# Attention of a metaformer layer: SyncE's loads put in another order, score tables in quarters, and the row maximum of three pieces in eight subtracted on GpSimd

## The chip, the cores and the metric

One core of one Trainium2 chip runs the whole layer as one program. The metric is the device time of one launch, in microseconds. Names of the engines in the profile: PE is TensorE's matmuls, PEld its weight loads, DVE is VectorE, ACT is ScalarE, POOL is GpSimd, SP is SyncE, whose queue issues nearly all transfers of this stage.

## What is computed

The layer normalises x over its last axis, adds an axial attention of 16 heads over the width, and adds a mixture of experts. The change is in the attention alone. For each of the 4 images, 16 heads and 128 rows i there is a 128 x 128 matrix of weights over j and w:

```
qk = jnp.einsum('nhcij,nhciw->nhijw', q, k) / D
qrq = jnp.einsum('nhcij,chjw->nhijw', q, rq) / D
krk = jnp.einsum('nhcij,chjw->nhijw', k, rk) / D
weight = jax.nn.softmax(qk + Gq * qrq + Gk * krk, axis=3)
out = jnp.einsum('nhijw,nhciw->nhcij', weight, Gv1 * v) + jnp.einsum('nhijw,chjw->nhcij', weight, Gv2 * rv)
```

The softmax runs over j. The tables rq, rk and rv belong to a head, so they change only when the head changes.

## The kernel before

Five stages run one after the other: prepare, project (it writes q, k and v to memory), attend (this case), combine, experts.

attend works in units. A unit is 64 rows of one image for one head, so a head has 8 units (k = 0 to 7) and there are 128 in all. A unit's scores lie in one of four buffers `scores0` to `scores3`, with w on the partitions. A unit is done in 8 turns (p = 0 to 7), one piece of 8 rows each, and several units are in hand at once. In a turn

- PE first does the own scores of piece p of unit u (`att_own`, L592), mixed with one round of relative scores from the tables (`att_rs` times `att_qk`, L581). These are for unit u + 1 while p < 6, and for unit u + 2 after that. Then come the sums with v (L622) and with rv (L634) for an earlier unit: u - 2 in turns 0 to 3, and u - 1 in turns 4 to 7;
- DVE adds the own scores to the relative ones and takes the row's extreme, negated (`add_and_largest`, L732, eight instructions). Two turns later it sums the exponentials of a piece (L715) and inverts the sums (L717);
- ACT takes exponentials of the piece before, row by row, with that row's `negmax` as its bias (`exp_half`, L675, eight instructions a piece). Then it copies the round of relative scores from PSUM into the buffer (`read_relative`, L668), and in every odd turn it copies a finished block of sums with rv out of PSUM (`read_r`, L682);
- POOL multiplies a piece by its inverse (`normalise`, L770).

The orders are written out by hand, and two waits matter most. PE's relative scores of a turn go into two banks of PSUM that ACT must have emptied (`rel_read`) before the next turn begins. `read_r` waits until PE has ended its odd turn (`r_done`).

SP issues in `unit` (L509 to L543): the second half of `att_own` for this unit, `att_qk` for two units ahead, the stores of unit u - 2, `att_vt` for unit u - 1, the first half of `att_own` for the next unit, and so on. PE needs the first `att_vt` at turn 4. In unit k = 6 SP also loads the next head's tables: 8 small loads of gains, then `att_rs` in two halves of 8 transfers each. A half can be overwritten only when PE has read it for unit 7. POOL multiplies each half by the gains (`scale_relative`, L765) before PE may use it. PE needs the first half at turn 6 of unit 6, and the second at turn 2 of unit 7.

Of the kernel before, what the change touches and what calls it, by code (L numbers as in the profile page):

```python
# [387 lines left out]
PR = 8  # L388
# [7 lines left out]
STORES_R = W // JT  # L396


def attend(nc, d):


    with ExitStack() as ctx:
# [12 lines left out]
        rs_loaded = [s.sem(f"rs_loaded{a}") for a in range(2)]  # L415
        rs_ready = [s.sem(f"rs_ready{a}") for a in range(2)]
# [8 lines left out]
        cleared = s.sem("cleared")  # L425
# [22 lines left out]
        def _(sp):  # L448
# [3 lines left out]
            def load_relative(h, a):  # L452
                for g in range(G):
                    for t in range(2):
                        at = slice(32 * g + HD * t, 32 * g + HD * t + HD)
                        j = g * JG + a * (JG // 2)
                        sp.dma_start(rs[at, a * (JG // 2):(a + 1) * (JG // 2), :].rearrange("c j w -> c (j w)"),
                                     tables[t][:, bass.ds(h, 1), j:j + JG // 2, :].rearrange("c h j w -> (c h) (j w)")).then_inc(rs_loaded[a], 16)
# [46 lines left out]
            def unit(h, k, u, started, left):  # L505
                if started >= 1:
                    sp.wait_ge(own_done, PIECES * u)
                    load_own(h, k, 1)
                if left >= 2:  # L509
                    sp.wait_ge(rel_done, ROUNDS * u + ROUNDS)  # L510
                    load_qk(*after(h, k, 2))
                if started >= 2:
                    store(*before(h, k, 2), u - 2, 0)
                if started >= 1:
                    ph, pk = before(h, k, 1)
# [6 lines left out]
                fresh = k == UPH - 2 and left >= 2  # L522
                if fresh:
                    load_gain(h + 1)
                    sp.wait_ge(rel_done, ROUNDS * u + ROUNDS + ROUNDS // 2)
                    load_relative(h + 1, 0)
                if left >= 1:
                    sp.wait_ge(own_done, PIECES * u + PIECES // 2)
                    load_own(*after(h, k, 1), 0)
                if started >= 1:  # L530
                    later(sp, v_done, FILLS * (u - 1))
                    load_v(ph, pk, 1)
                    if pk == 0:
                        later(sp, r_done, FILLS * (u - 1))
                        load_rv(ph, 2)
                        load_rv(ph, 3)
                if started >= 2:
                    store(*before(h, k, 2), u - 2, 1)
                if fresh:
                    sp.wait_ge(rel_done, ROUNDS * u + 2 * ROUNDS)  # L540
                    load_relative(h + 1, 1)

            load_gain(0)  # L543
            for a in range(2):
                load_relative(0, a)
# [3 lines left out]
            for half in range(2):  # L549
                load_own(0, 0, half)  # L550
            for k in range(UPH):
                unit(0, k, k, k, 2)
            with sp.Fori(1, NH - 1) as h:
                for k in range(UPH):
                    unit(h, k, UPH * h + k, 2, 2)
# [15 lines left out]
        def _(pe):  # L571
            def before_relative(u, v, t):
                if t == 0:
                    pe.wait_ge(qk_loaded[v % 2], 64 * (u // 2) + 64)
                if t % (ROUNDS // 2) == 0:
                    pe.wait_ge(rs_ready[t // (ROUNDS // 2)], u // UPH + 1)
                later(pe, rel_read, ROUNDS * u + t)
# [83 lines left out]
        def _(act):  # L661
# [15 lines left out]

            def read_r(u, b):
# [5 lines left out]
            def unit(u, v, parts):  # L684
                back2, back1, now, ahead1, ahead2 = parts
                for p in range(PIECES):
# [13 lines left out]
                    if p % 2 and p >= 4 and back1:  # L700
                        read_r(u - 1, p // 2 - 2)

# [57 lines left out]
        def _(pool):  # L760
            def scale_relative(h, a):
                half = slice(a * (JG // 2), (a + 1) * (JG // 2))
                pool.wait_ge(rs_loaded[a], 128 * h + 128)
                pool.wait_ge(gain_loaded, 128 * h + 128)
                pool.tensor_tensor(rs[:, half, :], rs[:, half, :], gain[:, :].unsqueeze(2).broadcast_to([P, JG // 2, W]), ALU.mult).then_inc(rs_ready[a], 1)  # L765
# [7 lines left out]
            def head(h, last):  # L773
                for k in range(UPH):
                    for p in range(PIECES):
                        if k == UPH - 2 and not last and p == 3:
                            scale_relative(h + 1, 0)
                        if k == UPH - 2 and not last and p == 7:
                            scale_relative(h + 1, 1)
                        normalise(UPH * h + k, k % BUFS, p)  # L780

            for a in range(2):
                scale_relative(0, a)
            with pool.Fori(0, NH - 1) as h:
                head(h, False)
            head(NH - 1, True)
# [553 lines left out]
```

## Time and profile before

| | |
|---|---|
| median of 3 runs | 7852.92 us (7848.76 to 7871.15) |
| the profiled execution | 7833.53 us, span of its instructions 7831.8 us |
| attend, first to last turn | 1575 to 6184 us of the span |
| busy over the span | PE 83%, PE's weight loads 64%, DVE 68%, ACT 60%, POOL 32% |

The profiled execution is 19 us below the median. The rows quoted later give the start in us from the start of the span, then the length in us, then engine, line, operation and tiles, and at the end in brackets how long the engine stood idle before and what ended that. Matmuls of one kind that follow each other are merged into one row with their count (two records for each matmul of the source). The relative and own scores alternate, so they make many short rows, of which only the first of a turn is shown.

### The profile page before, as it was taken

To read this page: it belongs to the slowest core of one execution; us is meant where nothing else is said; L and a number is where in the kernel's file an instruction comes from. 1 tells how busy PE (TensorE), PEld (TensorE's weight loads), DVE (VectorE), ACT (ScalarE), POOL (GpSimd) and SP (SyncE) were. 2 spreads that over 40 slices of the span, in tenths; PEclk is the share of its full clock that TensorE was granted. 3 is DMA by queue.
4 is the path that set the end of the run, shared out by engine and by line. 5 is a ranking of instruction groups with operands and counts; after the bars stand their busy time and mean duration, and the time that the engine had idled before them with its cause. 6 is when DMAs were issued, how large, how long until landed. Compare 5 with 4: busy or idle time off the path is not lost. (4 is left out here: it accounts for less than half of the span.)

```text
span 7831.8 us, 282296 instructions
## 1 busy us (share of the span) xinstructions
PE 6488.4 (83%) x106442; PEld 5044.5 (64%) x106442; DVE 5358.1 (68%) x20905; ACT 4715.2 (60%) x11171; POOL 2470.2 (32%) x1235
## 2 busy tenths in 40 slices
PE   4999999788898888888898888888888776675648
PEld 3555555477777777777777777777777632232248
DVE  5444444267787777777777777777777698888830
ACT  0444444277787787787787787787787533343310
POOL 0000000034444444444444444444444432232210
PEclk7999999879999999999999999999999998897855
DMA  7555555546656566666656656666666686686522
GB/s 220 202 204 203 203 204 202 147 90 119 117 114 121 112 116 118 114 115 120 113 114 121 114 113 122 112 115 120 111 115 120 148 266 194 202 263 198 177 92 91
DMA packets 1861132, 1148.19 MB, mean 147 GB/s; under 512 B 1162209, under 2 KB 1623649, under 8 KB 1853601
## 3 DMA queue, kind: packets, MB, share of 16 engines
q1 hardware_dynamic: 1670368, 842.63, 49.2%
q10 hardware_dynamic: 188352, 285.27, 10.0%
q8 instruction: 834, 13.66, 0.8%
q14 instruction: 554, 4.53, 0.2%
q0 software_dynamic: 1024, 2.09, 0.1%
HBM read 708.04 MB, written 421.56 MB: 144 GB/s over the span
## 5 line engine op out<-in xcount | busy, mean ns | idle before, releaser
L770 POOL TENSOR_TENSOR att_scores<-att_scores,att_inverse 128x1024 f32<-128x1024 f32 x1024 | 1989.5, 1943 | 2452.0 <-DVE att_inverse L717 2452.0
L732 DVE CUSTOM_DVE_ANT_0 att_scores<-att_ps,att_scores 128x128 f32<-128x128 f32 x8192 | 1819.2, 289 | 1158.7 <-PE att_ps L592 1120.5
L675 ACT ACTIVATE att_scores<-att_scores,att_negmax 128x128 f32<-128x128 f32 x8192 | 2515.0, 394 | 74.7 <-issue 69.5
L581 PE MATMUL att_ps<-att_qk,att_rs 32*128 32x64 f32 x32768 | 2253.6, 300 | 50.8 <-DMA att_qk<-qk 40.5
L592 PE MATMUL att_ps<-att_own 32*128 32x128 f32 x16384 | 1859.1, 328 | 401.3 <-POOL att_rs L765 179.4
L592 PEld LDWEIGHTS att_ps<-att_own 32*128 32x128 f32 x16384 | 1657.3, 197 | 712.4 <-issue 463.3
L581 PEld LDWEIGHTS att_ps<-att_qk,att_rs 32*128 32x128 f32 x32768 | 2073.5, 200 | 52.8 <-issue 43.6
L668 ACT ACTIVATE att_scores<-att_ps 128x1024 f32<-128x1024 f32 x1024 | 1033.7, 1010 | 609.3 <-PE att_ps L581 608.6
L634 PE MATMUL att_ps<-att_scores,att_rv 128*16 128x64 f32 x32768 | 1384.5, 332 | 9.3 <-DMA att_rv<-rv_t 6.3
L715 DVE TENSOR_REDUCE att_total<-att_scores 128x8 f32<-128x1024 f32 x1024 | 1241.5, 1212 | 0.0
L634 PEld LDWEIGHTS att_ps<-att_scores,att_rv 128*16 128x16 f32 x32768 | 1130.9, 121 | 35.1 <-DMA att_rv<-rv_t 12.1
L366 PE MATMUL proj_qk_ps<-proj_xn,proj_w_qk 128*128 128x512 f32 x2048 | 902.5, 594 | 33.4 <-DVE proj_xn L230 33.4
L622 PE MATMUL att_ps<-att_scores,att_vt 128*16 128x128 f32 x16384 | 692.2, 290 | 214.1 <-DMA att_vt<-v_t 182.6
L890 PE MATMUL comb_y_ps<-comb_att,comb_wo 128*128 128x512 f32 x1024 | 510.9, 657 | 220.9 <-DVE comb_x L931 193.5
L366 PEld LDWEIGHTS proj_qk_ps<-proj_xn,proj_w_qk 128*128 128x128 f32 x2048 | 390.2, 191 | 470.3 <-issue 463.8
L732 DVE DVE_READ_ACCUMULATOR2_ANT att_negmax<- 128x1 f32 x8192 | 688.6, 84 | 0.1
L335 ACT ACTIVATE proj_qk_out<-proj_qk_ps 128x512 f32<-128x512 f32 x512 | 305.1, 596 | 625.7 <-PE proj_qk_ps L366 616.7
L765 POOL TENSOR_TENSOR att_rs<-att_rs,att_gain 128x2048 f32<-128x2048 f32 x32 | 115.3, 3604 | 1640.4 <-DMA att_rs<-in_L_conv_rk_dram 1640.4
L622 PEld LDWEIGHTS att_ps<-att_scores,att_vt 128*16 128x16 f32 x16384 | 374.7, 99 | 336.3 <-issue 218.1
L872 POOL TENSOR_TENSOR comb_att<-comb_sum_v,comb_sum_r 128x1024 f32<-128x1024 f32 x128 | 329.0, 2590 | 819.9 <-DMA comb_x<-in_x_dram 739.2
L890 PEld LDWEIGHTS comb_y_ps<-comb_att,comb_wo 128*128 128x128 f32 x1024 | 209.6, 210 | 527.0 <-issue 274.2
L682 ACT ACTIVATE att_att_r<-att_ps 128x512 f32<-128x512 f32 x512 | 305.8, 597 | 370.1 <-PE att_ps L634 370.0
(147 smaller groups left out, 5173.6 us busy)
## 6 DMA issues: line engine op xcount, KB each, us to landing
qk<-proj_qk_out ACTq DMA_DIRECT2D x64, 2048.0 KB, 8.6
att_qk<-qk SPq DMA_DIRECT2D x512, 256.0 KB, 5.9
att_own<-qk SPq DMA_DIRECT2D x2048, 64.0 KB, 2.5
proj_x<-in_x_dram SPq DMA_DIRECT2D x128, 512.0 KB, 4.3
v_t<-proj_v_out ACTq DMA_DIRECT2D x64, 1024.0 KB, 11.7
att_vt<-v_t SPq DMA_DIRECT2D x256, 256.0 KB, 3.3
att_v<-att_att_v SPq DMA_DIRECT2D x1024, 64.0 KB, 2.5
att_r<-att_att_r SPq DMA_DIRECT2D x1024, 64.0 KB, 2.1
```

The costliest lines, as they stand in the source:

```text
L366: last = pe.matmul(qk_ps[:, j], w_qk[:, a, 4 * j:4 * j + 4].rearrange("c h t e -> c (h t e)"), xn[u][:, a, sub * BANK:(sub + 1) * BANK], s ...
L581: return pe.matmul(ps[:, 4 + gg, jj * IU:(jj + 1) * IU], rs[32 * g:32 * g + 32, j, :], qk[v % 2][32 * g:32 * g + 32, :, j], start=True, st ...
L592: return pe.matmul(ps[:, g, r * W:(r + 1) * W], own[half][32 * g:32 * g + 32, 1, at, :], own[half][32 * g:32 * g + 32, 0, at, :], start=Tr ...
L622: last = pe.matmul(ps[32 * g:32 * g + HD, 6, r * W:(r + 1) * W], vt[i // HROWS][:, i % HROWS, :], scores[v % BUFS][:, i, :], start=True, s ...
L634: last = pe.matmul(ps[32 * g:32 * g + HD, 7, jj * IU:(jj + 1) * IU], rv[:, j, :], scores[v % BUFS][:, :, j], start=True, stop=True, tile_p ...
L668: act.activation(scores[o % BUFS][:, :, :].rearrange("w i (g j) -> w i g j", g=G)[:, :, pair:pair + 2, t // 2 * JB:(t // 2 + 1) * JB], ps[ ...
L675: last = act.activation(scores[v % BUFS][:, i, :], scores[v % BUFS][:, i, :], ACT.Exp, bias=negmax[v % BUFS][:, i:i + 1], scale=-1.0)
L715: dve.tensor_reduce(total[v][:, rows], scores[v][:, rows, :], AX_X, ALU.add).then_inc(summed, 1)
L732: last = dve.tensor_tensor_reduce(out=scores[v][:, i, :], in0=ps[:, 2 * (p % 2) + r // HR, (r % HR) * W:(r % HR + 1) * W], in1=scores[v][: ...
L770: pool.tensor_tensor(scores[v][:, rows, :], scores[v][:, rows, :], inverse[v][:, rows].unsqueeze(2).broadcast_to([P, PR, W]), ALU.mult).th ...
L872: pool.tensor_tensor(att[u][:, a, :].rearrange("c (i g j) -> c i g j", i=ROWS, g=STORES_R), sum_v[u][:, a, :].rearrange("c (i g j) -> c i ...
L890: last = pe.matmul(y_ps[:, b], wo[:, a, o * P:(o + 1) * P], att[u][:, a, sub * BANK:(sub + 1) * BANK], start=a == 0, stop=a == CHALF - 1)
```

## The change

It has three parts.

1. In SP's order the first `att_vt` comes right behind the first `att_own`, ahead of the stores. `att_qk` moves from the start of the unit to its end, and is loaded for three units ahead.
2. The tables come in quarters, each loaded as soon as PE has done with the old one, and each multiplied by the gains on its own.
3. For pieces 0, 2 and 4 of every unit POOL subtracts the scores from the row extreme (`shift`), and ACT then takes one exponential over the whole piece (`exp_shifted`) in place of eight. These come at the end of ACT's turn, behind `read_r`. POOL's `normalise` runs two pieces behind.

```diff
@@ sync: unit
+                ahead = ROUNDS * (u + 1)
+                fresh = k == UPH - 2 and left >= 2
                 if started >= 1:
+                    ph, pk = before(h, k, 1)
                     sp.wait_ge(own_done, PIECES * u)
                     load_own(h, k, 1)
-                if left >= 2:
-                    sp.wait_ge(rel_done, ROUNDS * u + ROUNDS)
-                    load_qk(*after(h, k, 2))
-                if started >= 2:
-                    store(*before(h, k, 2), u - 2, 0)
                     later(sp, v_done, FILLS * (u - 2) + FILLS // 2)
                     load_v(ph, pk, 0)
...
                 if fresh:
                     load_gain(h + 1)
-                    sp.wait_ge(rel_done, ROUNDS * u + ROUNDS + ROUNDS // 2)
+                    sp.wait_ge(rel_done, ahead + 2)
                     load_relative(h + 1, 0)
+                if started >= 2:
+                    store(*before(h, k, 2), u - 2, 0)
+                if fresh:
+                    sp.wait_ge(rel_done, ahead + 4)
+                    load_relative(h + 1, 1)
...
+                if left >= 3:
+                    sp.wait_ge(rel_done, ahead + ROUNDS)
+                    load_qk(*after(h, k, 3))
@@ scalar
+            def exp_shifted(u, v, p):
+                rows = slice(p * PR, (p + 1) * PR)
+                act.wait_ge(shifted, len(SHIFTED) * u + SHIFTED.index(p) + 1)
+                act.activation(scores[v % BUFS][:, rows, :], scores[v % BUFS][:, rows, :], ACT.Exp, scale=-1.0).then_inc(exped, 2)
...
-                    elif now:
+                    elif now and p - 1 not in SHIFTED:
                         exp_half(u, v, 2 * p - 2)
                         exp_half(u, v, 2 * p - 1)
...
+                    if now and p - 1 in SHIFTED:
+                        exp_shifted(u, v, p - 1)
@@ gpsimd
+            def shift(u, v, p):
+                rows = slice(p * PR, (p + 1) * PR)
+                pool.wait_ge(added, HALVES * u + 2 * p + 2)
+                pool.tensor_tensor(scores[v][:, rows, :], scores[v][:, rows, :], negmax[v][:, rows].unsqueeze(2).broadcast_to([P, PR, W]),
+                                   ALU.subtract).then_inc(shifted, 1)
+            def head(h, first, last):
+                for k in range(UPH):
+                    u = UPH * h + k
                     for p in range(PIECES):
+                        if k == UPH - 2 and not last and p % 2 == 1:
+                            scale_relative(h + 1, p // 2)
+                        if p in SHIFTED:
+                            shift(u, k % BUFS, p)
+                        if p >= BEHIND:
+                            normalise(u, k % BUFS, p - BEHIND)
+                        elif k or not first:
+                            normalise(u - 1, (k - 1) % BUFS, PIECES + p - BEHIND)
```

ACT's order in unit 2, whose scores are `att_scores2`, from the `read_r` (L682) of turn 1 to that of turn 3. Before:

```order
L682 ACTIVATE att_att_r1<-att_ps 128x64x8
L675 ACTIVATE att_scores2<-att_scores2,att_negmax2 128x128 x8
L668 ACTIVATE att_scores3<-att_ps 128x64x2x8
L675 ACTIVATE att_scores2<-att_scores2,att_negmax2 128x128 x8
L668 ACTIVATE att_scores3<-att_ps 128x64x2x8
L682 ACTIVATE att_att_r1<-att_ps 128x64x8
```

And in the changed kernel, where `read_r` is L697, `exp_half` L685, `read_relative` L678 and `exp_shifted` L691:

```order
L697 ACTIVATE att_att_r1<-att_ps 128x64x8
L691 ACTIVATE att_scores2<-att_scores2 128x1024
L685 ACTIVATE att_scores2<-att_scores2,att_negmax2 128x128 x8
L678 ACTIVATE att_scores3<-att_ps 128x64x2x8 x2
L697 ACTIVATE att_att_r1<-att_ps 128x64x8
```

Before, one group of eight exponentials stood in each turn, ahead of its `read_relative`. Now both exponentials of a pair of turns stand between `read_r` and the `read_relative` of the even turn, and none stands in the odd turn.

POOL in unit 6, from the first to the last multiplication of the tables (L782), where L787 is `normalise` and L793 `shift`, in the changed kernel:

```order
L782 TENSOR_TENSOR att_rs<-att_rs,att_gain 128x1024
L787 TENSOR_TENSOR att_scores<-att_scores,att_inverse 128x1024
L793 TENSOR_TENSOR att_scores<-att_scores,att_negmax 128x1024
L787 TENSOR_TENSOR att_scores<-att_scores,att_inverse 128x1024
L782 TENSOR_TENSOR att_rs<-att_rs,att_gain 128x1024
L787 TENSOR_TENSOR att_scores<-att_scores,att_inverse 128x1024
L793 TENSOR_TENSOR att_scores<-att_scores,att_negmax 128x1024
```

Before, POOL had two such multiplications of 128 x 2048 in this unit, in turns 3 and 7, and only `normalise` around them; now there are four of 128 x 1024, in turns 1, 3, 5 and 7, and the `shift` of pieces 2 and 4 stands behind the first two.

## Rows read from the trace of the kernel before

**Rows 1.** ACT in a regular stretch, order of time (turn pair without stall).

```profile
2721.09 0.60 ACT L682 ACTIVATE att_att_r<-att_ps 128x512 f32<-128x512 f32 x1 [0.71 <-PE att_ps L634]
2721.58 2.47 ACT L675 ACTIVATE att_scores<-att_scores,att_negmax 128x128 f32<-128x128 f32 x8
2723.95 1.00 ACT L668 ACTIVATE att_scores<-att_ps 128x1024 f32<-128x1024 f32 x1
2724.85 2.43 ACT L675 ACTIVATE att_scores<-att_scores,att_negmax 128x128 f32<-128x128 f32 x8
...
2728.92 0.60 ACT L682 ACTIVATE att_att_r<-att_ps 128x512 f32<-128x512 f32 x1 [0.73 <-PE att_ps L634]
```

**Rows 2.** PE in the same stretch: sums with v (L622), with rv (L634).

```profile
2719.68 1.35 PE L634 MATMUL att_ps<-att_scores,att_rv 128*16 128x64 f32 x32
...
2723.39 1.34 PE L634 MATMUL att_ps<-att_scores,att_rv 128*16 128x64 f32 x32
2725.00 0.37 PE L592 MATMUL att_ps<-att_own 32*128 32x128 f32 x1 [0.28 <-ACT att_scores L668]
...
2726.97 0.63 PE L622 MATMUL att_ps<-att_scores,att_vt 128*16 128x128 f32 x16
2727.42 1.35 PE L634 MATMUL att_ps<-att_scores,att_rv 128*16 128x64 f32 x32
```

**Rows 3.** Waits in attend, 1575 to 6184: us in total, times, longest.

```profile
PE att_ps L622 <- DMA att_vt<-v_t: 182.1, 74, 4.4
PE att_ps L592 <- POOL att_rs L765: 179.4, 30, 9.3
PE att_ps L592 <- ACT att_scores L668: 127.5, 362, 1.2
```

**Rows 4.** SP's queue in a unit 6: start, time to issue, count.

```profile
2654.75 4.17 SPq L477 DMA_DIRECT2D att_own<-qk  x7
2659.20 6.61 SPq L469 DMA_DIRECT2D att_qk<-qk  x4
...
2672.37 0.38 SPq L482 DMA_DIRECT2D att_vt<-v_t  x1
2672.93 3.62 SPq L464 DMA_DIRECT2D att_gain<-gain_t  x8
2676.80 0.32 SPq L457 DMA_DIRECT2D att_rs<-in_L_conv_rq_dram  x1
...
2681.40 0.37 SPq L457 DMA_DIRECT2D att_rs<-in_L_conv_rk_dram  x1
```

**Rows 5.** POOL in the same unit.

```profile
2686.55 3.60 POOL L765 TENSOR_TENSOR att_rs<-att_rs,att_gain 128x2048 f32<-128x2048 f32 x1 [7.88 <-DMA att_rs<-in_L_conv_rk_dram]
```

**Rows 6.** PE in the same unit: start of turn 3, then of turn 6.

```profile
2667.70 0.37 PE L592 MATMUL att_ps<-att_own 32*128 32x128 f32 x1 [0.26 <-ACT att_scores L668]
...
2690.29 0.57 PE L592 MATMUL att_ps<-att_own 32*128 32x128 f32 x1 [8.09 <-POOL att_rs L765]
...
2693.90 1.05 PE L622 MATMUL att_ps<-att_scores,att_vt 128*16 128x128 f32 x16
```

**Rows 7.** Groups of instructions, 1400 to 6600: count | busy us, mean ns | idle before.

```profile
L770 POOL TENSOR_TENSOR att_scores<-att_scores,att_inverse 128x1024 f32<-128x1024 f32 x1024 | 1989.5, 1943 | 2452.0 <-DVE att_inverse L717 2452.0
...
L668 ACT ACTIVATE att_scores<-att_ps 128x1024 f32<-128x1024 f32 x1024 | 1033.7, 1010 | 609.3 <-PE att_ps L581 608.6
...
L205 ACT ACTIVATE comb_ln_sq<-comb_ln_xc 128x2048 f32<-128x2048 f32 x19 | 36.3, 1910 | 88.7 <-DVE comb_ln_xc L201 86.2 <-issue 2.3
```

**Rows 8.** PE behind a wait of 1.25 us for v.

```profile
5541.72 0.63 PE L622 MATMUL att_ps<-att_scores,att_vt 128*16 128x128 f32 x16 [1.25 <-DMA att_vt<-v_t]
...
5545.41 0.63 PE L622 MATMUL att_ps<-att_scores,att_vt 128*16 128x128 f32 x16
```

**Rows 9.** PE behind a wait of 1.52 us for v.

```profile
4601.29 0.80 PE L622 MATMUL att_ps<-att_scores,att_vt 128*16 128x128 f32 x16 [1.52 <-DMA att_vt<-v_t]
...
4606.00 0.63 PE L622 MATMUL att_ps<-att_scores,att_vt 128*16 128x128 f32 x16
```

More of the change, by code:

```diff
@@ L414, in attend @@
         ps = s.ps("ps", [P, 8, BANK])
-        rs_loaded = [s.sem(f"rs_loaded{a}") for a in range(2)]
-        rs_ready = [s.sem(f"rs_ready{a}") for a in range(2)]
+        rs_loaded = [s.sem(f"rs_loaded{a}") for a in range(QUARTERS)]
+        rs_ready = [s.sem(f"rs_ready{a}") for a in range(QUARTERS)]
         qk_loaded = [s.sem(f"qk_loaded{b}") for b in range(2)]
@@ L536, in unit @@
                         load_rv(ph, 3)
+                if fresh:
+                    sp.wait_ge(rel_done, ahead + 6)
+                    load_relative(h + 1, 2)
                 if started >= 2:
@@ L539, in unit @@
                 if fresh:
-                    sp.wait_ge(rel_done, ROUNDS * u + 2 * ROUNDS)
-                    load_relative(h + 1, 1)
+                    sp.wait_ge(rel_done, ahead + 8)
+                    load_relative(h + 1, 3)
+                if left >= 3:
+                    sp.wait_ge(rel_done, ahead + ROUNDS)
+                    load_qk(*after(h, k, 3))
             load_gain(0)
-            for a in range(2):
+            for a in range(QUARTERS):
                 load_relative(0, a)
@@ L550, in _ @@
                 load_own(0, 0, half)
+            sp.wait_ge(rel_done, ROUNDS)
+            load_qk(0, 2)
             for k in range(UPH):
[L552 removed]
+                unit(0, k, k, k, 3)
             with sp.Fori(1, NH - 1) as h:
                 for k in range(UPH):
[L555 removed]
+                    unit(h, k, UPH * h + k, 2, 3)
             for k in range(UPH):
@@ L771, in normalise @@
                                    ALU.mult).then_inc(normed, 1)
-            def head(h, last):
+            def shift(u, v, p):
[3 more added lines that the diff above has]
+                                   ALU.subtract).then_inc(shifted, 1)
+            BEHIND = 2
+            def head(h, first, last):
                 for k in range(UPH):
+                    u = UPH * h + k
                     for p in range(PIECES):
[L776 to L782, printed above, removed]
-                scale_relative(0, a)
-            with pool.Fori(0, NH - 1) as h:
-                head(h, False)
-            head(NH - 1, True)
+                        if k == UPH - 2 and not last and p % 2 == 1:
[6 more added lines that the diff above has]
+                            normalise(u - 1, (k - 1) % BUFS, PIECES + p - BEHIND)
+            for a in range(QUARTERS):
+                scale_relative(0, a)
+            head(0, True, False)
+            with pool.Fori(1, NH - 1) as h:
+                head(h, False, False)
+            head(NH - 1, False, True)
+            for p in range(PIECES - BEHIND, PIECES):
+                normalise(UNITS - 1, (UPH - 1) % BUFS, p)
 def combine(nc, d):
```

21 lines of the change are left out of this document (10 added, 11 removed).

## Prediction

> **What bounds the kernel now.** The change touches attend alone, 4,609 of 7,832 us, so I read that stage turn by turn. In a regular pair of turns ACT's timeline shows this order [rows 1]: `read_r` at 2721.09, exponentials at 2721.58, `read_relative` at 2723.95, exponentials at 2724.85, and `read_r` again at 2728.92, for which it waited 0.73 us for PE. PE's timeline shows the other side [rows 2]: its sums with rv start at 2719.68, 2723.39 and 2727.42. So the odd turn gives way to the even one after 3.71 us, and the even one to the next after 4.03 us. At 2725.00, which begins the next turn, PE had waited 0.28 us for ACT's `read_relative`. The reader is to see a loop of two engines: PE ends an odd turn, ACT does `read_r`, the exponentials and `read_relative`, and only then may PE begin the turn after next. The start of `read_r` to the end of `read_relative` is 2724.95 - 2721.09 = 3.86 us. A bit over 0.1 us at the two hand-overs, and PE's turn of 3.70 us, fit under the same roof, so both engines are nearly bound, and it matters on which side of `read_r` a piece of ACT's work stands.
>
> A unit without stalls is four pairs of 4.06 + 3.70 us, or 31.1 us, and 128 of them 3,980 us. The stage takes 4,609. The list of waits says where most of the rest goes [rows 3]: PE waited 182 us in 74 places for `att_vt`, and 179 us in 30 places for the tables. Each longer wait costs more than itself. After one for the tables PE is at the lower of its two clock levels, 1.2 GHz where it has 2.4 otherwise: the scores of the turn take 2693.90 - 2690.29 = 3.61 us [rows 6], where 2726.97 - 2725.00 = 1.97 us is regular [rows 2], and with the sums with v behind them the turn is about 2.0 us longer. After a wait of 1.52 us for v the sums with v follow each other at 4.71 us [rows 9], 1.0 us over the 3.69 that a wait of 1.25 us left behind it [rows 8].
>
> **Part 1, SP's order.** SP is a serial queue that takes time to issue. In a unit 6 [rows 4] `att_own` is issued by 2659.2, then `att_qk` takes 6.6 us, the stores take until 2672.4, and only then `att_vt` goes, at 2672.37. Without the 13 us between, it goes at 2659.2, 13 us sooner, and the longest wait for it was 4.4 us. I take all of the 182 us as gone, and with them the slow scores, about 65 us (some 65 of the 74 waits at 1.0 us, an estimate from rows 8 and 9). Gain: 247 us. What becomes late instead: `att_qk` goes at turn 5 and is used at turn 6 of the next unit, over 30 us later. The stores are needed a unit later. SP's issues of a regular unit come to at most 30 us (twice `att_own` at 4.7, `att_qk` at 6.6, twice the stores at up to 6.6, 0.8 for v, all from rows 4), below its 31 to 34 us. I count nothing.
>
> **Part 2, tables in quarters.** The first quarter can be overwritten before unit 6 begins, and goes behind `att_own`, `att_vt` and the gains. From the times in rows 4 I take out the 13.2 us of `att_qk` and stores: gains at 2659.7, the quarter issued from 2663.6 to some 2668, landed by 2670.2 to 2673.3 (POOL got the half 5.1 us after the last issue [rows 4, 5]; the quarter has half the bytes, so 2.2 to 5.1). PE needs it only at turn 6, 17 us on. The three others come one to every two turns, each with as much room. The 179 us go, and with them 30 slow turns at 2.0 us, 60. Gain: 239 us.
>
> POOL, though, is an engine with one order. The multiplication of the first quarter stands in turn 1, and behind it wait one `normalise` and the `shift` of piece 2. With 1.94 us for each operation on 128 x 1024 [rows 7] the three end 5.8 us behind the landing, between 2676.0 and 2679.1. ACT wants it after `read_r` of turn 3: that turn began at 2667.70 before [rows 6], 0.93 us later now (below), and 3.7 + 0.5 us bring it to 2672.8. So ACT, and PE behind it, stand 3.2 to 6.3 us in every unit 6. I take 3.2, the near end, since these loads then have the transfers to themselves, and 1.0 us for the slow scores behind it: 15 x 4.2 = 63 us back. The GPSIMD Engine Reference of the Trainium skill, section 3.1, measures 4.50 us for a two-input operation of 2048 elements; here 3.60 us is measured [rows 5], and the measurement decides. By the page's figure three operations at half would take 6.7 us in place of 5.8, and the sum would be 14 us higher. Sixteen more issues by SP at the start of the stage, about 0.5 us each, are partly under the transfers: 4 us.
>
> **Part 3, the wide exponential.** ACT's work falls: eight exponentials take 2.37 us from start to start [rows 1], and one over 1024 elements should take about 0.93 us. I take the copy of 1024 elements, 1.01 us long and 0.90 to the next start [rows 1, 7]; half of the square over 2048 with its fixed part, also 1.04 us [rows 7], less 0.1 of overlap, gives 0.94. Ends: 0.85 and 1.05. Three pieces save 4.3 us of ACT in a unit.
>
> But ACT is not short of time where these pieces go. They leave the odd turn, where ACT then only waits longer for PE, and come to stand behind `read_r`, ahead of the exponentials and the `read_relative` that PE waits for. The path from PE's end of an odd turn to its start of the turn after next grows from 4.06 by the whole wide exponential to 4.99 us, in turns 2, 4 and 6. PE's wait there grows from 0.28 to 1.21 us. Nothing covers it: PE's work in the turn is 3.70 us. The saved 2.37 us lie in turns that PE bounds at 3.70, and give nothing. So 3 x 0.93 x 127 units = 354 us are lost (ends 324 and 400). The `shift` itself adds 3 x 1.94 us to POOL's 8 x 1.94, under 22 of 34 us. Outside unit 6 it waits only for DVE's addition of the same turn, and ACT wants it at the end of the next, so some 2 us of room are left and it costs nothing; without that room its own 1.94 us would be on the path, up to the hold of unit 6.
>
> **The clock.** Will 381 new waits of 1.21 us bring PE's clock down? A wait of 1.25 us did not: the next turn is 3.69 us [rows 8]. One of 1.52 us did [rows 9]. The new one is under this line by little, and it lies beside the scores and not between scores and sums. I take one in four as followed by a lower level, at 0.3 us each, since most of the slow work then falls into the next wait: 30 us. Ends: 0, and one in two at 0.6, 114 us. The Trainium skill, TensorE: Matmul & The Clock Gate, in the section on a second failure mode (psum-queue depth-cycling), says that frequent short idles of PE between groups, without one long idle, make the clock go up and down. That speaks against this change, and by that rule the costly end would hold.
>
> **Sum.** -247 - 239 + 63 + 4 + 354 + 30 = -35 us. That is 7,799 us against the profiled execution's 7,833.5. The runs' median is 19 us above it, so 7,853 - 35 = 7,818; I round to 7,815.
>
> **The rivals.**
>
> - *The wide exponential is not exposed.* If ACT's loop has slack that I don't see, or the wide one takes much less, the transfers' gain shows: -35 - 354 + part. With half exposed it is 7,640, with nothing exposed 7,460. For it: the transfers' stalls are large and real. Against it: the 0.28 us that PE waits already [rows 2]. Chance 0.10.
> - *The clock falls at the new waits.* One in two at 0.6 us gives 114 in place of 30 us: 7,900. At 1.0 us for every second, as behind the wait of 1.52 us, it is 7,978. Slower from the point where the mean cost of a new wait passes 0.17 us (65/381). Chance 0.16.
> - *POOL's order holds ACT longer in unit 6.* At 6.3 us in place of 3.2 it costs 47 us more: 7,862, no difference. It becomes slower only with a second hold in the same unit. Chance 0.10.
> - *The loads are not earlier* because SP or the transfer engines are full. If half of the waits for v stay, it is +120 us: 7,935. Against it: the 13 us of room. Chance 0.04.
> - The forecast, 7,740 to 7,875: 0.60.
>
> **How the numbers follow.** 0.3% is 24 us, about what can be told from no change. In the forecast's own range, two thirds lie below -24 us, most of the rest within it. Faster: 0.60 x 0.66 + 0.10 = 0.50. Slower: 0.16 + 0.04 + 0.02 + a few hundredths of the forecast = 0.25. Same: 0.25. The range from 7,725 to 7,910 leaves out the first rival and the worst of the second and fourth, about 2 in 10.
>
> **What would show it.** Right: PE's rows for v follow each other at 4.99 and 3.70 us in turns 2 to 7; PE's wait for `read_relative` ahead of the own scores goes from 127 us in total [rows 3] to nearly 500; waits for `att_vt` and the tables are gone; POOL waits for the table's load in turn 1 of unit 6, and ACT for POOL two turns on; ACT's busy time is down by 500 us with no gain from it. Wrong: even turns at 4.06 us, a granted clock in regular units that is well under 1.00, or a new wait on a DMA in units 6 and 7.

## The result, and the profile after it

The changed kernel takes 7925.77 us (median of 4 runs, 7911.08 to 7927.84), the kernel before in the same session 7850.84 us (4 runs, 7842.32 to 7871.15). The ratio is 1.0088, interval 1.0065 to 1.0111: 75 us slower by the medians, where 35 us faster was forecast, and 16 us above the end of the stated range. Attend alone moved: from 4609.5 us to 4691.2 us in the profiled executions. The page's line of busy times, after:

```profile
PE 6529.8 (83%) x106442; PEld 5094.0 (64%) x106442; DVE 5360.0 (68%) x20905; ACT 4212.9 (53%) x8483; POOL 3177.3 (40%) x1651
```

ACT works 502 us less than before (4715.2) and POOL 707 us more (2470.2), and neither shows in the time. The list of waits in attend, 1575 to 6266 (us in total, times, longest), answers to [rows 3]:

```profile
PE att_ps L602 <- ACT att_scores L678: 517.0, 456, 4.4
...
POOL att_rs L782 <- DMA att_rs<-in_L_conv_rk_dram: 228.9, 60, 10.3
PE att_ps L602 <- issue: 108.6, 29, 4.7
ACT att_scores L691 <- POOL att_scores L793: 82.7, 25, 6.7
...
PE att_ps L632 <- POOL att_scores L787: 25.6, 12, 3.6
...
PE att_ps L602 <- DMA att_own<-qk: 0.5, 1, 0.5
```

The first column is the total, the second the number of waits. The waits for `att_vt` (182 us) and for the multiplied tables (179 us) are gone. PE's wait for `read_relative` went from 127.5 to 517.0 us. ACT now waits for `shift`, 82.7 us. PE in a regular stretch, the sums with rv (L644) and the first own scores of a turn, answers to [rows 2]:

```profile
2679.33 1.34 PE L644 MATMUL att_ps<-att_scores,att_rv 128*16 128x64 f32 x32
2680.95 0.37 PE L602 MATMUL att_ps<-att_own 32*128 32x128 f32 x1 [0.28 <-ACT att_scores L678]
...
2683.38 1.35 PE L644 MATMUL att_ps<-att_scores,att_rv 128*16 128x64 f32 x32
...
2687.08 1.35 PE L644 MATMUL att_ps<-att_scores,att_rv 128*16 128x64 f32 x32
2689.68 0.37 PE L602 MATMUL att_ps<-att_own 32*128 32x128 f32 x1 [1.25 <-ACT att_scores L678]
...
2692.10 1.34 PE L644 MATMUL att_ps<-att_scores,att_rv 128*16 128x64 f32 x32
```

Turn 0 of unit 6 still has the old order: from its sums with rv (2679.33) to those of the next turn (2683.38) it is 4.05 us, with the old wait of 0.28 us between. From turn 2, the next even one, with a wide exponential (2687.08), it is 5.02 us (2692.10), with a wait of 1.25 us. ACT in the same stretch and on through the stall of unit 6, which answers to [rows 1] (`read_r` L697, `exp_shifted` L691, `exp_half` L685, `read_relative` L678):

```profile
2684.79 0.60 ACT L697 ACTIVATE att_att_r<-att_ps 128x512 f32<-128x512 f32 x1 [0.71 <-PE att_ps L644]
2685.28 1.05 ACT L691 ACTIVATE att_scores<-att_scores 128x1024 f32<-128x1024 f32 x1
2686.23 2.49 ACT L685 ACTIVATE att_scores<-att_scores,att_negmax 128x128 f32<-128x128 f32 x8
2688.60 1.03 ACT L678 ACTIVATE att_scores<-att_ps 128x1024 f32<-128x1024 f32 x1
2691.77 1.02 ACT L678 ACTIVATE att_scores<-att_ps 128x1024 f32<-128x1024 f32 x1 [2.14 <-PE att_ps L591]
2693.51 0.60 ACT L697 ACTIVATE att_att_r<-att_ps 128x512 f32<-128x512 f32 x1 [0.72 <-PE att_ps L644]
2700.83 1.08 ACT L691 ACTIVATE att_scores<-att_scores 128x1024 f32<-128x1024 f32 x1 [6.72 <-POOL att_scores L793]
```

From `read_r` at 2684.79 to the end of `read_relative` at 2689.63 it is 4.84 us, where it was 3.86. In the odd turn ACT now idles 2.14 us: most of the 2.37 us that were saved there, used by nobody. Then comes the hold that was forecast at 3.2 us. It is 6.72 us long here, the longest of the heads 1 to 14, which have 3.3 to 6.7 us and 5.2 in the mean. What led to it stands in SP's queue and on POOL:

```profile
2668.84 6.04 SPq L471 DMA_DIRECT2D att_qk<-qk  x4
2675.22 7.06 SPq L479 DMA_DIRECT2D att_own<-qk  x8
2682.53 0.35 SPq L484 DMA_DIRECT2D att_vt<-v_t  x1
2683.05 4.70 SPq L466 DMA_DIRECT2D att_gain<-gain_t  x8
2688.04 0.32 SPq L459 DMA_DIRECT2D att_rs<-in_L_conv_rq_dram  x1
...
2691.66 1.11 SPq L459 DMA_DIRECT2D att_rs<-in_L_conv_rk_dram  x1
```

```profile
2695.11 1.89 POOL L782 TENSOR_TENSOR att_rs<-att_rs,att_gain 128x1024 f32<-128x1024 f32 x1 [10.27 <-DMA att_rs<-in_L_conv_rk_dram]
2696.96 1.90 POOL L787 TENSOR_TENSOR att_scores<-att_scores,att_inverse 128x1024 f32<-128x1024 f32 x1
2698.82 1.93 POOL L793 TENSOR_TENSOR att_scores<-att_scores,att_negmax 128x1024 f32<-128x1024 f32 x1
```

`att_qk` now stands right ahead of the own load of the next unit. Here the eight issues of `att_own` take 7.06 us, where seven took 4.17 [rows 4], and the gains take 4.70 for 3.62. Over the stage, the eight issues of `att_own` right behind `att_qk` take 6.3 us in the middle (42 places, with 8 of 10 between 5.7 and 7.2), and 4.1 us right behind `att_vt` in the kernel before (66 places). PE begins its next turn at 2705.20, after 4.02 us without work.

To add this up I took, for each turn, the time from its first own scores to those of the next turn, as a mean over heads 1 to 14, by unit (k) and turn. Before and after, the units that matter:

```
        turn 0     1     2     3     4     5     6     7
before k2  4.06  3.70  4.05  3.70  7.08  3.98  4.15  3.69
after  k2  4.07  3.70  5.03  3.81  5.03  3.78  5.10  3.71
before k3  4.06  3.70  4.05  3.70  6.21  4.24  4.15  6.95
after  k3  4.09  3.70  5.03  3.77  5.02  3.76  5.10  7.25
before k6  4.06  3.70  4.05  3.70  6.27 13.30  5.74  3.88
after  k6  4.07  3.70  5.02  3.96 10.34  5.57  5.09  3.75
before k7  4.05  7.17  4.89  3.98  4.06  3.70  4.15  6.99
after  k7  4.14  3.70  5.60  4.56  4.93  3.77  5.10  7.87
before k0  4.35  3.99  4.13  3.70  4.21  3.70  4.15  3.69
after  k0  5.53  4.18  5.10  3.96  5.03  3.76  5.09  3.83
```

Summed over a head it is 289.85 us before and 295.36 after, 5.5 us more. By parts, in us a head: waits for v -15.6; tables -16.0; wide exponential +23.1 (24 even turns at 0.95 to 0.98); turns 4 and 5 of unit 6 +7.2; turns 2 to 4 of unit 7 +1.3; the turns at the jumps of the loop (turn 7 of units 3 and 7, turns 0 and 1 behind them) +2.7; small excesses of other turns, most of them odd turns behind a wait of 1.2 us, +2.7.

### The profile page after: what moved, and what is told of

Same layout as the page of the kernel before. It is cut to its first block and busy times, and to the rows that moved or that the text cites. A ratio compares the mean times of both kernels' runs of the same rounds, so it can differ in the third digit from the quotient of the medians.

```text
span 7909.4 us, 281112 instructions
## 1 busy us (share of the span) xinstructions
PE 6529.8 (83%) x106442; PEld 5094.0 (64%) x106442; DVE 5360.0 (68%) x20905; ACT 4212.9 (53%) x8483; POOL 3177.3 (40%) x1651
## 3 DMA queue, kind: packets, MB, share of 16 engines
q0 software_dynamic: 1024, 2.09, 0.1%
## 5 line engine op out<-in xcount | busy, mean ns | idle before, releaser
L787 POOL TENSOR_TENSOR att_scores<-att_scores,att_inverse 128x1024 f32<-128x1024 f32 x1024 | 1987.0, 1942 | 1449.1 <-DVE att_inverse L734 1449.0
L602 PE MATMUL att_ps<-att_own 32*128 32x128 f32 x16384 | 1890.8, 332 | 627.9 <-ACT att_scores L678 517.0
L591 PE MATMUL att_ps<-att_qk,att_rs 32*128 32x64 f32 x32768 | 2292.8, 303 | 50.5 <-DMA att_qk<-qk 39.9
L602 PEld LDWEIGHTS att_ps<-att_own 32*128 32x128 f32 x16384 | 1688.6, 200 | 943.2 <-ACT att_scores L678 633.9
L591 PEld LDWEIGHTS att_ps<-att_qk,att_rs 32*128 32x128 f32 x32768 | 2112.4, 204 | 52.7 <-issue 46.2
L685 ACT ACTIVATE att_scores<-att_scores,att_negmax 128x128 f32<-128x128 f32 x5120 | 1580.1, 398 | 80.9 <-issue 80.4
L678 ACT ACTIVATE att_scores<-att_ps 128x1024 f32<-128x1024 f32 x1024 | 1038.4, 1014 | 1042.4 <-PE att_ps L591 1042.2
L644 PE MATMUL att_ps<-att_scores,att_rv 128*16 128x64 f32 x32768 | 1383.7, 332 | 1.9 <-ACT att_att_r L697 1.9
L644 PEld LDWEIGHTS att_ps<-att_scores,att_rv 128*16 128x16 f32 x32768 | 1140.2, 122 | 20.6 <-issue 3.1
L793 POOL TENSOR_TENSOR att_scores<-att_scores,att_negmax 128x1024 f32<-128x1024 f32 x384 | 730.6, 1903 | 277.8 <-DVE att_negmax L749 274.5
L782 POOL TENSOR_TENSOR att_rs<-att_rs,att_gain 128x1024 f32<-128x1024 f32 x64 | 122.5, 1914 | 1740.1 <-DMA att_rs<-in_L_conv_rk_dram 1740.1
L922 PEld LDWEIGHTS comb_y_ps<-comb_att,comb_wo 128*128 128x128 f32 x1024 | 210.0, 210 | 520.7 <-issue 269.0
L697 ACT ACTIVATE att_att_r<-att_ps 128x512 f32<-128x512 f32 x512 | 306.0, 598 | 431.2 <-PE att_ps L644 431.2
```

What stands on the lines that cost most here:

```text
L591: return pe.matmul(ps[:, 4 + gg, jj * IU:(jj + 1) * IU], rs[32 * g:32 * g + 32, j, :], qk[v % 2][32 * g:32 * g + 32, :, j], start=True, st ...
L602: return pe.matmul(ps[:, g, r * W:(r + 1) * W], own[half][32 * g:32 * g + 32, 1, at, :], own[half][32 * g:32 * g + 32, 0, at, :], start=Tr ...
L644: last = pe.matmul(ps[32 * g:32 * g + HD, 7, jj * IU:(jj + 1) * IU], rv[:, j, :], scores[v % BUFS][:, :, j], start=True, stop=True, tile_p ...
L678: act.activation(scores[o % BUFS][:, :, :].rearrange("w i (g j) -> w i g j", g=G)[:, :, pair:pair + 2, t // 2 * JB:(t // 2 + 1) * JB], ps[ ...
L685: last = act.activation(scores[v % BUFS][:, i, :], scores[v % BUFS][:, i, :], ACT.Exp, bias=negmax[v % BUFS][:, i:i + 1], scale=-1.0)
L787: pool.tensor_tensor(scores[v][:, rows, :], scores[v][:, rows, :], inverse[v][:, rows].unsqueeze(2).broadcast_to([P, PR, W]), ALU.mult).th ...
```

## The experiments

"Head" is the sum over a head as above. Each ratio is to the kernel before in the same session, with its interval. The kernel before had a median of 7850.84 us beside the changed kernel, 7840.49 beside e1 to e4, 7841.73 beside e5 to e8, and 7837.36 beside e9 to e11. So where two versions of different sessions are compared, the text takes the difference of each from the kernel before of its session.

| run | median us | ratio | head us | regular turns 2, 4, 6 |
|---|---|---|---|---|
| before | 7837 to 7851 | 1 | 289.85 | 4.05 |
| changed kernel | 7925.77 | 1.0088 (1.0065 to 1.0111) | 295.4 | 5.03 |
| e1 | 7642.19 | 0.9739 (0.9717 to 0.9762) | 278.4 | 4.06 |
| e2 | 8069.65 | 1.0280 (1.0255 to 1.0306) | 305.5 | 5.03 |
| e3 | 7682.48 | 0.9792 (0.9770 to 0.9814) | 280.5 | 4.25 |
| e4 | 7932.76 | 1.0111 (1.0088 to 1.0135) | 296.4 | 5.03 |
| e5 | 7899.96 | 1.0075 (1.0060 to 1.0090) | 294.4 | 5.03 |
| e6 | 7597.28 | 0.9687 (0.9673 to 0.9700) | 275.8 | 4.05 |
| e7 | 7567.80 | 0.9649 (0.9634 to 0.9663) | 274.3 | 3.70 |
| e8 | 7642.44 | 0.9737 (0.9722 to 0.9752) | 278.3 | 4.05 |
| e9 | 7483.81 | 0.9550 (0.9529 to 0.9571) | 269.0 | 3.70 |
| e10 | 7501.28 | 0.9570 (0.9542 to 0.9597) | 268.6 | 4.05 |
| e11 | 7821.90 | 0.9982 (0.9969 to 0.9994) | 289.4 | 5.03 |

### Transfers alone, the exponential alone

e1 is the changed kernel with no shifted piece, so all exponentials are eight narrow ones again:

```diff
-SHIFTED = (0, 2, 4)
+SHIFTED = ()
```

> The changed kernel without its third part: no piece is shifted on GpSimd, all exponentials are again row by row in their old place, the order of SyncE and the quarters stay. Theory (the wide exponential stands on the path from read_r to read_relative): even turns are back at 4.06 us, the waits for v and the tables stay away, only GpSimd's hold in unit 6 is left. 7926 - 370 (three times 0.97 us in 127 units) - some 40 of slow scores behind the new waits, up to 100 less if the hold of unit 6 goes with the shift: 7,420 to 7,520 us. Rival (the transfers gave little, the time is lost in units 6 and 7 and in the order of SyncE): 7,800 or more.

Measured: 7642.19 us, 198 us faster than before, and so 273 us better than the changed kernel, which is 75 us slower. The even turns are back at 4.06 us. It missed its range, since turn 3 of unit 7 takes 12.39 us and turn 4 of unit 6 takes 9.75. The waits of e1 say for what:

```profile
POOL att_rs L782 <- DMA att_rs<-in_L_conv_rk_dram: 364.1, 60, 13.1
...
PE att_ps L602 <- DMA att_own<-qk: 128.1, 15, 10.9
...
PE att_ps L632 <- POOL att_scores L787: 83.2, 15, 6.8
```

The wait for `att_own` is new. It is 0.5 us in the changed kernel, whose longer turns give SP time.

e2 is the other half: the kernel before with the shift and the wide exponentials. With them go `normalise` two pieces behind, as in the change, and the two multiplications of the table halves two turns later (turn 5 of unit 6 and turn 1 of unit 7). Only ACT's part of the edit is shown:

```diff
+SHIFTED = (0, 2, 4)
-                    elif now:
+                    elif now and p - 1 not in SHIFTED:
+                    if now and p - 1 in SHIFTED:
+                        exp_shifted(u, v, p - 1)
```

> The kernel before with the third part alone: pieces 0, 2 and 4 are shifted on GpSimd and get one wide exponential at the end of ScalarE's turn; SyncE's order and the tables in halves are those of before. Theory: 7851 + 370 + some 40 for slow scores, 8,220 to 8,270 us, even turns at 5.03 us. Rival (the parts hide each other, the new wait is taken up in the waits for v): below 8,100 us, since the waits for v at turn 4 would take in the later turns.

Measured: 8069.65 us, 229 us slower than before, below the expected range and where the rival put it. The even turns are 5.03 us long. The wait for `att_vt` fell to 80 us from 182, since longer turns gave that load more time; turn 4 of unit 1 was 3.2 us over its regular length before and is 1.8 over it here. Alone the halves are -198 and +229 us, which adds up to +31, and together they are +75. A part of what each load gains by coming sooner, the longer turns give it anyway.

### The wide exponential on the other side of `read_r`

In e3 only the place in the turn changes:

```diff
+                    if now and p - 1 in SHIFTED:
+                        exp_shifted(u, v, p - 1)
                     if p % 2 and p < 4 and back2:
                         read_r(u - 2, 2 + p // 2)
                     if p % 2 and p >= 4 and back1:
                         read_r(u - 1, p // 2 - 2)
-                    if now and p - 1 in SHIFTED:
-                        exp_shifted(u, v, p - 1)
```

> The changed kernel with the wide exponential moved ahead of read_r in the same turn; its length and GpSimd's work stay. Theory (its place costs, not its length): ScalarE has about 0.65 us free ahead of read_r, so only some 0.3 us of each 0.95 stay on the path. Even turns 4.35 us in place of 5.03: 7926 - 381 x 0.67 - some of the slow scores = 7,640 to 7,680 us. Rival (GpSimd's extra work, or the shift that comes late, slows the turns): 7,900 us, since both are as before.

Measured: 7682.48 us, 158 us faster than before, and so 233 us better than the changed kernel. That is 2 us above the expected range. ACT in e3:

```profile
2458.82 1.02 ACT L678 ACTIVATE att_scores<-att_ps 128x1024 f32<-128x1024 f32 x1 [2.15 <-PE att_ps L591]
2459.74 1.13 ACT L691 ACTIVATE att_scores<-att_scores 128x1024 f32<-128x1024 f32 x1
2460.78 0.57 ACT L697 ACTIVATE att_att_r<-att_ps 128x512 f32<-128x512 f32 x1
2461.26 2.47 ACT L685 ACTIVATE att_scores<-att_scores,att_negmax 128x128 f32<-128x128 f32 x8
```

The wide exponential lies where ACT stood idle for PE. `read_r` starts without idle time ahead of it, so it is still some 0.2 us late: the turn takes 4.25 us, not 4.05. The same instructions, moved by one place, are worth 233 us.

### Removing the stall of unit 6

In e4 POOL multiplies each quarter two turns later, behind the `shift` that ACT needs:

```diff
-                        if k == UPH - 2 and not last and p % 2 == 1:
-                            scale_relative(h + 1, p // 2)
+                        if k == UPH - 2 and not last and p in (3, 5, 7):
+                            scale_relative(h + 1, p // 2 - 1)
+                        if k == UPH - 1 and not last and p == 1:
+                            scale_relative(h + 1, 3)
```

> The changed kernel with GpSimd's four multiplications of the tables each two turns later (turns 3, 5 and 7 of unit 6, turn 1 of unit 7). Theory (GpSimd waits for the first quarter's load with the shift of piece 2 queued behind it): the wait in turn 4 of unit 6 (10.3 us against 5.0) and the slow turn behind it go, 7926 - 15 x 7 = 7,820 us, and about 20 less if the longer turns 2 and 3 of unit 7 go too. Rival (ScalarE waits there for the load or the stores themselves): no difference, 7,926 us.

Measured: 7932.76 us, 92 us slower than before where the changed kernel is 75 slower: no gain, and not the 7,820 that was expected. Turn 4 of unit 6 is 5.02 us for 10.34, so the hold is gone; and turn 3 of unit 7 is 12.26 us for 4.56. SP's queue in e4, from the end of the last quarter:

```profile
2715.22 0.37 SPq L459 DMA_DIRECT2D att_rs<-in_L_conv_rk_dram  x1
2715.77 6.83 SPq L471 DMA_DIRECT2D att_qk<-qk  x4
2722.79 4.46 SPq L479 DMA_DIRECT2D att_own<-qk  x8
```

And PE waits for that last load:

```profile
2730.05 0.57 PE L602 MATMUL att_ps<-att_own 32*128 32x128 f32 x1 [8.70 <-DMA att_own<-qk]
```

In this head (head 3) the issues of that load end 56.5 us after the start of unit 6, and 56.0 us after it in the changed kernel, so SP is no later. PE comes to the load 50.6 us after that start in place of 60.3: the hold of unit 6 had given SP the time in which it caught up. In units 6 and 7 of the changed kernel, from issue to issue with no gap over 0.45 us, SP works for 78.6 of 81.2 us (mean of 14 heads). In the kernel before it was 72.6 of 83.7 us. SP is nearly full in these two units, and a stall that is removed in one place comes up at the next load.

e5 is e4 with the last quarter and `att_qk` of unit 6 issued in unit 7, behind the loads that are needed first:

```diff
+                if behind:
+                    sp.wait_ge(rel_done, ahead)
+                    load_relative(h + 1, 3)
+                    load_qk(*after(h, k, 2))
...
-                if fresh:
-                    sp.wait_ge(rel_done, ahead + 8)
-                    load_relative(h + 1, 3)
-                if left >= 3:
+                if left >= 3 and not fresh:
```

> As the run with the multiplications of the tables two turns later, and the last quarter of the tables and att_qk of unit 6 now go in unit 7, behind its att_own and att_vt. Theory (SyncE's queue is what is short in units 6 and 7: with the hold on GpSimd gone, att_own of unit 7 comes too late because the last quarter and att_qk stand ahead of it): the turn of 12.3 us and the slow one behind it go, 9.6 us in each of 15 heads, 7933 - 144 = 7,770 to 7,800 us. Rival (the transfers themselves are what is full there, and another one comes late in its place): 7,900 us or more.

Measured: 7899.96 us, 58 us slower than before, some 34 us better than e4 where 130 or more was expected, and so where the rival put it. Turns 3, 4 and 5 of unit 7 take 7.17, 8.02 and 5.22 us, now because the last quarter is late: POOL waits 8.14 us for it in the same head, and PE waits 43.4 us in 14 places for POOL's product. Another order helps a full queue little. e6 and e7 are e5 with no shifted piece, and with pieces 1, 3 and 5 in place of 0, 2 and 4. Then the wide exponential stands in the even turn, ahead of the odd turn's group of eight, where ACT is idle, and not between `read_r` and `read_relative`:

```diff
-SHIFTED = (0, 2, 4)
+SHIFTED = ()  # e6
...
+SHIFTED = (1, 3, 5)  # e7
```

> The same order of SyncE and of the tables, without the shift and the wide exponential. Theory: the transfers alone are then worth what was forecast for parts 1 and 2, since both long turns of the run with the transfers alone go (6.4 and 11.0 us over a regular turn pair, 15 heads, 260 us): 7642 - 260 = 7,380 to 7,410 us. Rival (one of the two stays or moves): 7,450 to 7,550 us.

> The same again with the shift and the wide exponential, but for pieces 1, 3 and 5 in place of 0, 2 and 4: the wide exponential then ends the even turn, where ScalarE is not behind read_r, and read_relative of the even turn comes right behind read_r. Theory (what counts is how much ScalarE has to do between read_r and the read_relative of the next turn): turns 2, 4 and 6 go from 4.05 us to PE's own 3.7 to 3.8, 7390 - 127 x 1.0 = 7,250 to 7,290 us. Rival (VectorE, whose work of a pair of turns is 7.1 to 7.4 us, bounds the turns then, or GpSimd's shift comes too late): 7,370 us or more.

Measured: 7597.28 and 7567.80 us, both slower than expected: e6 lies above both its range and its rival's, e7 where its rival put it. In e7 turns 2, 4 and 6 take 3.70 us, PE's own work, and turns 3, 5 and 7 take 3.75. So wide exponentials can shorten the loop of ACT and PE. Of the 127 us that this was to bring, e7 won 29 against e6, and the rest is given back: turn 3 of unit 7 takes 13.03 us and turn 5 of unit 6 11.25, and ACT waits 257.8 us for `shift`.

### The jump of the loop

The loops of PE, ACT and DVE hold four units and jump back after units 3 and 7. There PE waits for nothing that the profile shows ("issue"): 93.2 us in 29 places before, 108.6 after, and the longest went from 3.5 to 4.7 us. The moved `att_qk` is in flight just then. e8 is e6 with `att_qk` at the start of the unit again, behind v (in unit 6 behind the first quarter):

```diff
+                if left >= 2 and not fresh:
+                    sp.wait_ge(rel_done, ahead)
                     load_qk(*after(h, k, 2))
...
-                if left >= 3 and not fresh:
-                    sp.wait_ge(rel_done, ahead + ROUNDS)
-                    load_qk(*after(h, k, 3))
```

> As the run with the reordered SyncE and no shift, but att_qk goes for two units ahead near the start of the unit, behind att_own and att_vt, where it does not run beside the jump back of PE's and ScalarE's loops. Theory (att_qk at the end of the unit slows the fetch of instructions behind the jump: the turn is 8.0 us there against 6.95 before): turn 7 of units 3 and 7 is back at 7.0 us, 28 x 1.0 and some slow scores less: 30 to 45 us below the other run. Rival (the longer turn has another cause): no difference.

Measured: turn 7 of unit 3 went from 7.92 (e6) to 7.19 us, the longest wait of this kind from 4.8 to 3.8 us. Turn 7 of unit 7, whose `att_qk` moved too, stayed at 7.43 us. As a whole e8 is 45 us slower than e6, where 30 to 45 us faster was expected, since `att_qk` is ahead of loads and stores that are needed sooner: ACT's wait for the store of `att_r` grows from 44.0 to 177.0 us. So at one of the two jumps 0.7 us went with the transfers beside it, and the other did not change. What ends these waits the profile does not show.

### Fewer transfers

e9 is the changed kernel with pieces 1, 3 and 5 shifted, as in e7, and the tables in two halves, 16 transfers a head in place of 32. The second half and `att_qk` of unit 6 go at the end of unit 6, and not in unit 7 as in e7. The gains are loaded in unit 2. That is 24 issues less in units 6 and 7. POOL still multiplies by quarters, behind the `shift`s:

```diff
-                        j = g * JG + a * JB
+                        j = g * JG + a * HALF
...
-                pool.wait_ge(rs_loaded[a], 128 * h + 128)
+                pool.wait_ge(rs_loaded[a // 2], 128 * h + 128)
...
+            SCALED = ((UPH - 2, 3), (UPH - 2, 4), (UPH - 2, 7), (UPH - 1, 0))
```

e10 is e9 without shifted pieces, and e11 is e9 with the pieces 0, 2 and 4 of the change.

> As the changed kernel, with pieces 1, 3 and 5 shifted; the tables are loaded in two halves again (16 transfers a head in place of 32), the first behind the stores and the second behind turn 5 of unit 6; the gains are loaded in unit 2; GpSimd multiplies quarters, in turns 3, 4 and 7 of unit 6 and turn 0 of unit 7, behind the shift. Theory (SyncE issues without a break over units 6 and 7, some 0.5 us for each transfer, and whatever stands last comes late): with 24 issues less in these two units the long turns of 11 to 13 us go. The run with pieces 1, 3 and 5 and the quarters had 21.5 us of excess in units 6 and 7 of each head; all gone is 7568 - 320 = 7,250 us, and half of it 7,400. Rival (the loads are late since the transfer engines are full there, or the multiplications hold the shift): 7,500 us or more.

> The same order of transfers without shift and wide exponential. Theory: parts 1 and 2 are then worth what the forecast gave them, 7850 - 470 = 7,370 to 7,420 us. Rival (SyncE's issues are not what is short): 7,550 us or more, as the two runs without a shift and with quarters (7,642 and 7,597).

> The same order of transfers with pieces 0, 2 and 4 shifted and the wide exponential behind read_r, as in the changed kernel. Theory: the place of the wide exponential costs 3 x 0.97 us in 127 units whatever the transfers do, and some 40 us of slow scores: 7,400 + 370 + 40 = 7,780 to 7,820 us. Rival (without late transfers to share with, the wide exponential costs less): below 7,700 us.

Measured: 7483.81, 7501.28 and 7821.90 us. e10 lies between its range and its rival's, e11 2 us above its range. e9 is the fastest: 354 us faster than before. The waits that are left in it:

```profile
PE att_ps L598 <- POOL att_rs L778: 66.4, 15, 7.7
PE att_ps L598 <- DMA att_own<-qk: 62.6, 24, 6.5
ACT att_scores L687 <- POOL att_scores L789: 57.0, 23, 4.3
```

Against e7, e9 won 80 us, where 168 to 318 was expected. Its units are shorter, and the same loads are late in more places (turn 3 of unit 3 takes 6.96 us, turn 5 of unit 6 8.46). SP is still full: it works for 72.9 of the 74.4 us of units 6 and 7. Between e9 and e10 there is no clear difference: the medians are 17 us apart, the runs overlap (7474.55 to 7494.22 and 7481.40 to 7506.47), and the sums over a head are 269.0 and 268.6 us. Three turns of each unit are 0.35 us shorter in e9 (some 8 us a head), and all of it goes into the late loads.

e11 differs from the changed kernel only in the transfers and in POOL's order of the multiplications, and is 90 us better (15 us faster than before, where the changed kernel is 75 us slower). The other pairs say the same: 80 us from e7 to e9 and 92 us from e6 to e10, though there the order in unit 7 changes too. No run separates the halves from the gains that moved to unit 2. e11 differs from e10 only in the shifted pieces, and is 321 us slower: the even turns alone are 24 x 0.97 us a head longer, or 370 us, and part of the holds of e10 is covered by the longer turns (turn 5 of unit 6 takes 6.28 us in e10 and 3.79 in e11).

## Why the prediction was wrong

**The main terms were right.** Waits for v and slow turns behind them: forecast -247, measured -15.6 x 16 = -250. Tables: -239, measured -16.0 x 15 = -240. The wide exponential behind `read_r` is exposed in full: forecast +354 at 0.93 us, measured +366 at 0.96 in the mean, and e3 and e11 show that it is the place and not the instruction that costs it. It is 1.05 us long and 0.95 to the next start at 2685.28; the square over 2048 with its fixed part [rows 7] was the better neighbour. The first rival (not exposed) is refuted. PE waits 517 us for `read_relative` where "nearly 500" was named. What carried the kernel from slightly faster to slower is smaller than these.

**The step that failed is the price of the moved and added transfers.** The sum put it at 63 us (and 4 at the start), and three terms of it were too small or missing:

- *Part 2, unit 6.* "I take 3.2, the near end, since these loads then have the transfers to themselves." They did not. By the means of 14 heads, counted from the start of unit 6, the eight issues of `att_own` took 5.7 us where 4.7 was read, those of the gains 4.7 where 3.6 was read, and the last issue of the first quarter went at 13.9 us where the forecast had some 12.1. The quarter landed 3.1 us after that issue in place of 2.2. So POOL began at 17.0 us in place of 14.3, and ACT, which wanted the `shift` at 17.5 in place of 16.9, stood 5.2 us in place of 3.2. With the slow work behind it turns 4 and 5 took 7.2 us more a head, 108 us for 63. The rival that named POOL's order was right in mechanism, at a chance of 0.10, and its 6.3 us lay nearer to the measured 5.2 than the 3.2 of the sum.
- *Part 1, SP.* "I count nothing" rested on a regular unit, 30 of 31 to 34 us. I did not add the 32 table transfers and 8 gains to units 6 and 7, where the queue has hardly a gap after the change. In the changed kernel itself unit 7 got only +1.3 us a head, 20 us in all. But e1, e4 and e5 show that much more was behind it: what is taken from one stall comes up at the next. Halves in place of quarters, with the gains in unit 2, are worth 90 us in the changed kernel (e11). That is most of the miss of 110 us, but not the same terms: e11 has no hold in turn 4 of unit 6 (5.11 us), for which the forecast had counted 63 us, and so its 15 us under the kernel before are not the forecast's 35 come true.
- *The jump of the loop* was in no term: +2.7 us a head, 43 us. Units 3 and 7 had it before. That it grew by transfers beside it is shown for turn 7 of unit 3 alone (e8, 7.92 to 7.19 us). For unit 7, and for the turns behind the jump, the cause stays open.

**The clock.** Forecast +30 us, one new wait in four followed by slower work at 0.3 us. The excess of other turns is 2.7 us a head, 43 us, so the likely case stood and the rival (114 us or more) did not. Of 252 odd turns away from the jumps and the stalls, 76 take over 3.75 us: 4.07 in the mean, with a mean granted clock of 0.75. The others take 3.70 at 1.00. In e1, without the new waits, 15 of 252 do. But the line that the forecast drew, that a wait of 1.25 us leaves the clock up and one of 1.52 us does not, is not what decides. Here are turn 3 of unit 2 in head 2, behind a wait of 1.26 us, and turn 3 of unit 6 in head 3, behind 1.25 us. The granted clock is the last column but two:

```profile
2248.90 0.37 PE L602 MATMUL att_ps<-att_own 32*128 32x128 f32 x1 [1.26 <-ACT att_scores L678]
2248.90:2253.10 4.20, 4.20 (x96) 3.64 (x97) 2.36 (x19) 1.02 (x1) 2.80 (x2) 0.71 0.24 53
2689.68:2693.38 3.70, 3.70 (x97) 3.31 (x97) 1.88 (x17) 1.02 (x1) 0.00 (x0) 1.00 0.40 99
```

The rule of the Trainium skill, TensorE: Matmul & The Clock Gate, in the section on depth-cycling, is that frequent short idles of PE between groups alone make the clock go up and down. The trace agrees in kind, with these 76 turns against 15, and gives it a small price here: 43 us over 381 new waits, about 0.1 us each.

The misses are 12 (exponential), 45 (unit 6), 20 (unit 7), 43 (jump) and 13 (clock), less 3 (v), 1 (tables) and 4 (the start, where the forecast's 4 us did not show). They come to 125 us, from -35 to +90. The stage is 82 us longer. The rest is heads 0 and 15, which the means leave out: together they grew by 4 us, where two mean heads would have by 11.

## What to carry to other kernels

Where two engines hand work to each other in a loop, ask of every moved piece on which side of the hand-over it stands; saved work on the idle side is worth nothing, and added work on the other is paid in full, even if the engine's total falls by 500 us. Sum a serial queue over its fullest stretch, not over the average one: when it is full there, finer transfers can cost more than their earlier start brings, and removing one stall shows the next. Of the edits made to the new queue, fewer and larger transfers moved the total most, by 80 to 92 us; the changes of order alone moved it by 34 to 46, one of them for the worse (e5 against e4, e6 against e1, e8 against e6).

## What was not expected of the hardware

- The time to issue goes with what went into the queue ahead: in the changed kernel eight loads of `att_own` took 6.3 us in the middle right behind `att_qk` (42 places), 5.6 behind it with a pause of 0.5 us or more between (85 places), and 4.6 behind the stores (97 places). A table's transfer is issued about every 0.5 us, whether it is a quarter (eight start from 2688.04 to 2691.66) or a half (in e9 eight from 2588.80 to 2592.45).
- At the jump of a loop of four units PE stood 93.2 us in 29 places before and 108.6 after, 3.2 and 3.7 us each time, and ACT 69.5 and 80.4 us.
- At the lower clock not all of PE's work was slower. In the turn at 2248.90 above, with a granted clock of 0.50 from 2250.97 to 2253.17, the sums with v take 1.06 us for 0.63, and the sums with rv behind them 1.37 for 1.35.
- POOL's subtraction with an operand repeated along the row takes 1903 ns for 128 x 1024, like its multiplication (1942 ns).
